# Experts layers: turned, weighed selections built by VectorE from repeated rows instead of by TensorE transposes

## The reference, cut to what matters

```
scores = einsum('BTC,CE->BTE', layernorm(x), gate_w)        # E = 8 experts
probs_et = transpose(softmax(scores), (0, 2, 1))
top_p, top_idx = top_k(probs_et, 64)                        # 64 tokens per expert and batch
xin = take_along_axis(x, top_idx)
y = gelu(xin @ w1[e]) @ w2[e]                               # 128 -> 512 -> 128
out = zeros.at[b_idx, top_idx].add(y * top_p)
```

## Time and profile before

| | |
|---|---|
| executions, us | 2262.53, 2264.82, 2267.56 |
| profiled execution, us | 2265.85 (its span 2264.1, clock granted on average 0.943) |
| PE busy | 2009.0 us, 89% of the span |
| DVE, ACT, POOL busy | 1573.0, 1174.4, 857.1 us |
| first experts block, first to last work | 643.7 to 855.3 us |
| second experts block, first to last work | 1107.2 to 1324.9 us |

### The profile page before, as it was taken

How to read it: one execution, slowest core, us unless ns; L and a number is a source line. 1 busy time by engine, 2 the same in 40 slices (tenths; PEclk the granted TensorE clock), 3 DMA queues, 4 the chain that set the end, 5 groups by cost and what they waited for, 6 DMA issues and landing times. The chain is left out here.

```text
span 2264.1 us, 55096 instructions
## 1 busy us (share of the span) xinstructions
PE 2009.0 (89%) x21847; PEld 1339.1 (59%) x21847; DVE 1573.0 (69%) x2826; ACT 1174.4 (52%) x1968; POOL 857.1 (38%) x1361
## 2 busy tenths in 40 slices
PE   5999999999979997999698979997599985479996
PEld 2666666666658994665498966664355542335553
DVE  5777778777866425667654447775689975769994
ACT  4444444444333334666433226666478875448874
POOL 4444544545434422344233424440244323333340
PEclk9999999999989997999799989999699997769998
DMA  5000000000000012443000214440334320123431
GB/s 173 1 1 2 1 1 1 2 1 2 1 7 5 16 42 73 123 116 98 5 1 1 57 38 124 117 117 19 87 105 117 108 61 0 44 81 112 119 108 51
DMA packets 157394, 121.18 MB, mean 54 GB/s; under 512 B 14113, under 2 KB 129713, under 8 KB 157141
## 3 DMA queue, kind: packets, MB, share of 16 engines
q1 hardware_dynamic: 157140, 117.65, 18.6%
HBM read 63.48 MB, written 54.12 MB: 52 GB/s over the span
## 5 line engine op out<-in xcount | busy, mean ns | idle before, releaser
L1269 DVE TENSOR_REDUCE l_group_mx<-maxima 128x4 f32<-128x1024 f32 x248 | 304.0, 1226 | 52.4 <-PE maxima L1056 50.9
L1194 ACT ACTIVATE l_group_pr<-scores 128x1024 f32<-128x1024 f32 x256 | 261.7, 1022 | 70.7 <-PE scores L1077 68.1
L2450 POOL TENSOR_TENSOR l_wide_tiles_sum<-l_wide_pr 128x256 f32<-128x256 f32 x256 | 180.8, 727 | 200.1 <-ACT l_wide_pr L2389 199.9
L2419 DVE RECIPROCAL l_wide_rc<-bank 128x256 f32<-128x256 f32 x128 | 224.1, 1751 | 6.1 <-PE bank L2346 4.4
L2389 ACT ACTIVATE l_wide_pr<-scores 128x512 f32<-128x512 f32 x256 | 139.0, 594 | 160.3 <-PE scores L2329 160.3
L2403 DVE TENSOR_REDUCE l_wide_mx<-maxima 128x2 f32<-128x512 f32 x248 | 159.2, 684 | 42.5 <-PE maxima L2309 42.4
L1269 DVE TENSOR_REDUCE l_slope_mx<-maxima 128x6 f32<-128x768 f32 x124 | 118.9, 959 | 65.6 <-PE maxima L1063 64.5
L2379 ACT ACTIVATE l_wide_qk<-bank 128x512 f32<-128x512 f32 x128 | 76.4, 597 | 155.5 <-PE bank L2293 155.5
L1269 DVE TENSOR_REDUCE l_rope_mx<-maxima 128x6 f32<-128x768 f32 x124 | 118.8, 958 | 43.8 <-PE maxima L1063 42.8
L1194 ACT ACTIVATE l_slope_pr<-scores 128x768 f32<-128x768 f32 x128 | 103.6, 810 | 75.0 <-PE scores L1084 74.9
L1097 PE MATMUL bank<-l_group_pr,va 128*32 128x256 f32 x2048 | 142.2, 397 | 0.0
(11 more groups left out here) (577 smaller groups left out, 4838.6 us busy)
## 6 DMA issues: line engine op xcount, KB each, us to landing
l_group_st<-stack_dram SPq DMA_DIRECT2D x128, 192.0 KB, 3.3
l_slope_st<-stack_dram SPq DMA_DIRECT2D x64, 192.0 KB, 3.7
l_rope_st<-stack_dram SPq DMA_DIRECT2D x64, 192.0 KB, 3.8
stack_dram<-l_group_parts SPq DMA_DIRECT2D x64, 192.0 KB, 2.3
stack_dram<-l_group_parts SPq DMA_DIRECT2D x64, 128.0 KB, 1.9
...
```

The source lines that it names most:

```text
L1194: act.activation(pr[:, i % AHEAD, :, 0:keys], Tp[:, :, 0:keys], ACT.Exp).then_inc(s["exps"], 1)
L1269: dve.tensor_reduce(mx[:, b % 2, :, :, i], max_bank(i, b)[:, :, 0:BLOCKS * keys].rearrange("p z (a k) -> p z a k", k=keys), AX.X, ALU.max, ...
L2419: own.done(dve.reciprocal(rc[:], Ob[i % 2][:, S:2 * S]))
L2450: pool.tensor_tensor(tiles_sum[:, i % 2, z, :], pr[:, i % 2, z, 0:S], pr[:, i % 2, z, S:2 * S], ALU.add).then_inc(s["added"], 1)
```

## The change

The turned selections are no longer transposed. The places (as bf16) and the probabilities of each half, 64 rows of 256 tokens each, are stored to DRAM (`rstore`). For each unit SP repeats its rows over 64 partitions each (`fetch`, four DMAs), and two DVE instructions (`build`, slots 6 and 8) compare the repeated places with the number of the partition and multiply with the probability. `turn`, `late` and the multiplications on POOL are gone. `gpt` and the two fetched tiles exist once, so a fetch waits for the builds of the unit before, and a build waits for the fetch and for the scatter of the unit before.

```diff
@@ expert_schedule
-    if n >= 0:
-        a.update({4: [("turn", 0)], 5: [("turn", 1)], 6: [("turn", 2)], 7: [("turn", 3)]})
-    late = {3: [("late", 0), ("late", 1)], 8: [("late", 2), ("late", 3)]} if n == 0 else {}
+    build = {6: [("build", 0)], 8: [("build", 1)]}
@@ experts, sync
+            def fetch(unit):
+                wait(sp, s["weighed"], 2 * unit)
+                for u in range(U):
+                    rows = slice((U * unit + u) * E8, (U * unit + u + 1) * E8)
+                    to = slice(u * CAP, (u + 1) * CAP)
+                    sp.dma_start(unit_place[to].rearrange("p e s -> p (e s)"),
+                                 K.place_dram[rows].rearrange("e s -> (e s)").partition_broadcast(CAP)).then_inc(s["fetched"], 16)
+                    sp.dma_start(unit_prob[to].rearrange("p e s -> p (e s)"),
+                                 K.prob_dram[rows].rearrange("e s -> (e s)").partition_broadcast(CAP)).then_inc(s["fetched"], 16)
+            for unit in range(3):
+                fetch(unit)
+            for i in range(2):
+                routed.sp(sp, "rstore", i)
+            fetch(3)
             following.sp_first(sp)
-            following.first("sp", sp, 5 * HOSTED)
+            fetch(4)
+            following.first("sp", sp, 5)
+            fetch(5)
+            following.first("sp", sp, 5)
+            fetch(6)
+            fetch(7)
@@ experts, tensor
-                    elif what in ("turn", "late"):
-                        if i == 0:
-                            pe.wait_ge(s["weighed"], weighed_t.add(4))
-                        for j in range(4):
-                            ins = pe.transpose(bank[:, j * P:(j + 1) * P], gp[...], K.ident[:])
-                        ins.then_inc(full[b], 1)
...
                         pe.wait_ge(s["kept"], kept_t.add(2))
+                        pe.wait_ge(s["weighed"], 2 * n)
@@ experts, scalar
+            act.activation(routed.greatest[:, 0:1], K.rstd[:, 0:1], ACT.Gelu)
             normed(act, 1).then_inc(s["xn"], 1)
-            routed.root(act)
@@ experts, vector
+                    elif what == "build":
+                        if i == 0:
+                            dve.wait_ge(s["fetched"], 16 * 2 * U * (n + 1))
+                            wait(dve, s["scattered"], n)
+                        of = slice(4 * i, 4 * i + 4)
+                        dve.scalar_tensor_tensor(gpt[:, of], unit_place[:, of], number[:], unit_prob[:, of],
+                                                 ALU.is_equal, ALU.mult).then_inc(s["weighed"], 1)
@@ Route
+    def root(self, pool):
+        pool.tensor_tensor(self.K.rstd[:, tiles], self.K.var[:, tiles], self.power[:], ALU.pow).then_inc(self.s["root"], 1)
+    def sp(self, sp, what, i):
+        if i == 0:
+            self.copied(sp, "rby", 0)
+            sp.dma_start(K.prob_dram[rows], self.work[0][0:64]).then_inc(s["kept_prob"], 16)
+        else:
+            sp.wait_ge(s["place16"], 1)
+            sp.dma_start(K.place_dram[rows], self.place16).then_inc(s["kept_place"], 16)
...
+            if i == 3:                                   # rtop.3
+                dve.wait_ge(s["kept_prob"], 16)
...                                                      # rplace.3
+            dve.tensor_copy(self.place16, self.place).then_inc(s["place16"], 1)
@@ ROUTE_IN_WIDE
-    (12, 1, "rby.0"),
-    (12, 2, "rtop.0"),
+    (14, 1, "rby.0"),
+    (15, 0, "rtop.0 rtop.1 rtop.2"),
@@ ROUTE_IN_EXPERTS
-    (-1, 3, "rstat.0 rnorm.0 rnorm.1"),
+    (0, 1, "rstat.0"),
```

More of the change, by code:

```diff
@@ L302, in norm @@
             if i == 0:
[L303 to L304 removed]
+                own.done(eng.memset(self.power[:], -0.5))
                 own.done(eng.memset(self.gate[:], 0.0))
@@ L316, in norm @@
                 own.done(eng.tensor_tensor(rstd, var, self.power[:], ALU.pow))
+                self.shifts(eng, tiles, own)
             else:
                 eng.sem_inc(s["var"], 1)
-                eng.wait_ge(s["root"], 1)
-                own.done(eng.reciprocal(rstd, rstd))
-            own.done(eng.tensor_tensor(shift, mean, rstd, ALU.mult))
-            eng.tensor_scalar(shift, shift, -1.0, None, ALU.mult).then_inc(s["norm"], 1)
+        elif what == "rshift":
+            eng.wait_ge(s["root"], 1)
+            self.shifts(eng, slice(NT * ROUTED * self.half, NT * ROUTED * (self.half + 1)), own)
         elif what == "runit":
@@ L508 @@
     (9, 3, "rback.0"),
-    (10, 5, "rstat.1"),
-    (10, 7, "rnorm.4"),
-    (11, 0, "rnorm.5"),
-    (11, 1, "rturn.2"),
-    (11, 5, "rnorm.6"),
-    (11, 6, "rnorm.7"),
-    (12, 1, "rturn.3"),
-    (12, 2, "rgate.1"),
-    (12, 3, "rback.1"),
-    (12, 5, "rsoft.0"),
-    (12, 7, "rsoft.1"),
-    (13, 1, "rby.0"),
-    (13, 5, "rtop.0"),
-    (13, 7, "rtop.1"),
-    (14, 0, "rtop.2"),
-    (14, 1, "rtop.3"),
-    (14, 5, "rtop.4"),
-    (14, 7, "rtop.5"),
-    (15, 0, "rtop.6"),
-    (15, 1, "rtop.7"),
@@ L529 @@
[L529 to L543 removed]
+    (12, 6, "rstat.1"),
+    (12, 7, "rnorm.4"),
+    (13, 0, "rnorm.5"),
+    (13, 1, "rturn.2"),
@@ new lines @@
+    (13, 5, "rnorm.6"),
+    (13, 6, "rnorm.7"),
+    (14, 1, "rturn.3"),
+    (14, 2, "rgate.1"),
+    (14, 3, "rback.1"),
+    (14, 5, "rsoft.0"),
+    (14, 7, "rsoft.1"),
+    (15, 1, "rby.0"),
+    (15, 1, "rtop.0 rtop.1"),
+    (15, 2, "rtop.2 rtop.3"),
+    (15, 3, "rtop.4 rtop.5"),
+    (15, 4, "rtop.6 rtop.7"),
+    (15, 5, "rtop.8 rtop.9"),
+    (15, 6, "rtop.10 rtop.11"),
+    (15, 7, "rtop.12 rtop.13"),
+    (16, 0, "rtop.14 rtop.15"),
+    (16, 1, "rplace.0 rplace.1 rplace.2 rplace.3"),
@@ L555 @@
-    (1, 3, "rback.1 rsoft.0"),
-    (1, 4, "rsoft.1"),
-    (1, 8, "rby.0"),
-    (2, 0, "rtop.0"),
-    (2, 0, "rtop.1"),
-    (2, 1, "rtop.2"),
-    (2, 1, "rtop.3"),
-    (2, 2, "rtop.4"),
-    (2, 2, "rtop.5"),
-    (2, 3, "rtop.6"),
-    (2, 3, "rtop.7"),
+    (0, 1, "rstat.0"),
+    (0, 2, "rroot.0"),
+    (0, 4, "rshift.0"),
+    (0, 5, "rnorm.0 rnorm.1"),
+    (0, 8, "rturn.0"),
+    (1, 0, "rnorm.2 rnorm.3"),
+    (1, 1, "rturn.1"),
+    (1, 2, "rnorm.4 rnorm.5"),
+    (1, 3, "rgate.0 rturn.2"),
@@ L566 @@
+    (1, 4, "rback.0"),
+    (1, 5, "rnorm.6 rnorm.7"),
+    (1, 7, "rturn.3"),
+    (1, 8, "rgate.1"),
+    (2, 0, "rback.1 rsoft.0"),
+    (2, 1, "rsoft.1"),
+    (2, 2, "rby.0"),
+    (2, 2, "rtop.0"),
+    (2, 2, "rtop.1"),
+    (2, 2, "rtop.2"),
+    (2, 3, "rtop.3"),
+    (2, 3, "rtop.4"),
+    (2, 3, "rtop.5"),
+    (2, 4, "rtop.6"),
+    (2, 4, "rtop.7"),
     (2, 4, "rtop.8"),
-    (2, 4, "rtop.9"),
+    (2, 5, "rtop.9"),
     (2, 5, "rtop.10"),
@@ L571 @@
     (2, 6, "rtop.13"),
-    (2, 7, "rtop.14"),
+    (2, 6, "rtop.14"),
     (2, 7, "rtop.15"),
-    (2, 8, "rplace.0 rplace.1 rplace.2 rplace.3 rslot.0"),
+    (2, 7, "rplace.0 rplace.1 rplace.2 rplace.3"),
+    (2, 8, "rslot.0"),
 ])
@@ L755, in narrow_walk @@
     routed = ROUTE_IN_SLOPE if kind == "slope" else {}
-    for n in range(-max(ahead), NB - min(ahead)):
+    last = max([NB - min(ahead)] + [n + 1 for n, _ in routed])
+    for n in range(-max(ahead), last):
         for j, slot in enumerate(at):
@@ L1729, in expert_schedule @@
             pieces += e.get(slot, [])
-        pieces += late.get(slot, [])
+        if do_b:
+            pieces += build.get(slot, [])
         if n < 0:
@@ L1921, in step @@
                     b, filling = bank_of(fill, what, i)
-                    if what in ROUTE_ON and what in ("rstat", "rnorm"):
+                    if what in ("rstat", "rnorm", "rshift"):
                         routed.norm(dve, what, i, routed.own_norm.on(dve))
@@ L1967, in _ @@
             pool.tensor_copy(count[:], count_i[:]).then_inc(s["counted"], 1)
+            pool.wait_ge(s["counted"], 2)
+            for u in range(U):
+                wait(pool, s["numbered"], u)
+                pool.iota(number_i[u * CAP:(u + 1) * CAP], pattern=[[1, 1]], base=0, channel_multiplier=1).then_inc(s["numbered"], 1)
+            pool.wait_ge(s["numbered"], U)
+            pool.tensor_copy(number[:], number_i[:]).then_inc(s["numbered"], 1)
             def step(n, par, do_a, do_b, do_e):
@@ L1989, in _ @@
             pool.wait_ge(s["in_three"], 1)
-            batches(pool, [onehot_t], step, UNITS)
+            batches(pool, [], step, UNITS)
 def recurrent(nc, K, name, W):
```

121 lines of the change are left out of this document (48 added, 73 removed).

## The result

| | before | after |
|---|---|---|
| executions, us | median 2265.41 (2262.53 to 2267.56, 4 runs) | median 2237.69 (2232.76 to 2238.64, 4 runs) |
| ratio to before | | 0.9874, 95% interval 0.9859 to 0.989 |
| profiled execution, us | 2265.85 (span 2264.1, clock 0.943) | 2238.64 (span 2236.9, clock 0.944) |

A forecast was written before the change was run, and what follows sets the result against it. The prediction took PE to bound plain experts steps, DVE step 2 and the attention ends. Its terms, -28.4 - 11.8 - 8.4 + 4.0 + 1.6 + 1.0 + 3.4 + 0.7 = -37.9, gave 2227 us from 2264.8; own range 2219 to 2236, with rivals 2213 to 2244.

The forecast's parts named there:

- its own signs of being wrong: Steps 3 and 4 don't shrink, PE waits for `weighed` at a scatter, or DVE waits for fetches outside steps 5 and 6.
- The transposes: Between down and up in both experts blocks: 0.444 us of PE per group, all counted as gain, -28.4 us.
- The fetches of steps 5 and 6: Issued on SP behind the hosted stacks, they may hold builds past their slot: +0.5 us per block, +1.0.
- Rival B: Fetches of steps 5 and 6 and the stacks sharing SP hold scatter, 4 us in four steps: 2243 us, chance 0.06.
- Start of a block: Statistics and root leave step -1, so ACT copies at once and the first `up` comes 5.9 us earlier: -11.8 for both.
- step 0: First step of each experts block: 26.3 us falls to 18.5; beyond the transposes, -4.2 per block, -8.4 us.
- rival C: Full clock from the first `up`, no wait in step 1, faster selections: 6 us more per block, 2215 us, chance 0.13.
- Step 1: Takes in 1.2 us of routing on PE and a 0.8 us wait for ACT's copy: +4.0 us for both blocks.
- Step 2: DVE's ranking chain starts later; first block's step 25.1 us against 26.1, +0.8 per block beside the transposes' gain, +1.6.
- End of `wide`: Fourteen rankings and a cast move into the last batch, so the last division ends later: +3.4 us.
- End of `slope`: Six rankings, `rby` and a cast go into a last batch where DVE idled: +0.7 us, 0 to 3.6.
- Rival A: Moved routing costs what it was meant to hide, in steps 1 and 2, attentions and start: 2244 us, chance 0.15.

The follow-up runs named there:

- no_turns: The kernel before with PE's transposes and their DVE copies left out, nothing in their place: 2228.8 us, 35.9 less than before.
- turns_back: The changed kernel with transposes and POOL's multiplications put back, no fetch or build, routing still late: 2257.8 us, 7.6 less than before.
- fetch_first: The changed kernel with the fetches of units 5 and 6 issued on SP ahead of the hosted stacks: 2228.8 us, 8.9 less than the changed kernel.
- wide_fetch: The changed kernel with each fetch DMA bringing half the first batch's rows to 128 partitions, same bytes; second batch gets the first's weights: 2229.1 us.
- stat_early: The changed kernel with POOL's piece of the hosted statistics in step 3 moved ahead of its splitting of the normed x: 2232.2 us.
- combined: The changed kernel with early fetches, POOL's early statistics and both builds of step 2 behind the places: 2217.6 us, 20.1 less than the changed kernel.
- old_route: The changed kernel with the second half's routing back at its old places from step -1, root staying on POOL: 2254.3 us, 16.7 more.
- route_tight: The changed kernel with routing's pieces one to three slots earlier and the ranking from slot 0 of step 2: 2243.5 us, 5.8 more.
- dense: The changed kernel with early fetches and POOL's early statistics, all sixteen rankings and the places together ahead of step 2's kept copy: 2225.1 us.
- weights_later: The combined kernel with hosted weights moved from step 2 to step 3 and constant rows issued behind unit 4's fetch: 2215.5 us, 2.1 less than combined.

## Why the forecast was right in kind and 11 us off in size

The range held (2213 to 2244) and the direction came from the named places, but the forecast's own case was 2227 (2219 to 2236), and two of its own signs of being wrong came: step 4 did not shrink, and PE waited for builds at scatters. That the sum is off by no more than 11 us is in part luck: the front of the blocks gained more than forecast, and what the transposes cost was underrated (35.9, not 28.4), while late builds and the attentions took more than that back.

1. **The transposes** (-28.4). The work on PE was sized rightly: 1.7 us less per plain step, 1.78 forecast. The sentence "they stand between down and up with nothing late behind them" failed on both sides. Before, their copies were part of a wait of PE at the end of step 3 (1.22 us and a lower clock), which went too. After, the builds, which replace them on DVE, were late enough to hold PE at two places of the first block and three of the second. no_turns gives 35.9 for the transposes with nothing in their place, turns_back 20.1 for the change of one for the other.
2. **The fetches of steps 5 and 6** (+1.0). This is the term that failed, the mis-sized one: fetch_first puts it at 8.9. Rival B had the mechanism and the place, with 0.06. Two numbers were wrong. A fetch took 10.1 us with nothing ahead of it and 11.8 behind the stacks, not 7.4. A row of a transfer to all 128 partitions was the measure for four to 64; by wide_fetch that is 1.9 of the 2.7 us, and 0.8 stay unexplained. The stacks ahead, which the forecast left out of the fetch's time, add the other 1.7. And the wait was priced by when the fetch lands, not by what stands behind the build on the in-order DVE: two builds, the kept copy, the selections of the next unit.
3. **A wait that was in the trace of before and not priced**: DVE stood 3.63 us behind POOL's piece at the end of step 3. With step 3 shorter it became 5.20, and the build behind it made it PE's: 5.4 us in the two steps 4, of which stat_early alone keeps 1.7 in the blocks and combined all.
4. **Start of a block** (-11.8) and **step 0** (-8.4 and its transposes): right in mechanism, 12.8 us for the starts of the blocks from first selection to first `up` (POOL's index rows, which the forecast counted here, stand before it and take back 0.7 per block), and 17.4 us for step 0 against 18.5. The granted clock is 1.00, 2.4 GHz, from the first `up` on, as rival C had it.
5. **Step 1** +0.7 against +0.4, with 0.50 us of PE's wait for the copy of `rgate.0` where 0.8 was taken. **Step 2**: 26.5 us against 25.1. The wait for the places was 3.99, not 2 to 3. While POOL split the normed x, a build took 1.45 us and one small piece 1.22, where in the second block they took 1.28 and 0.28, the small piece after POOL had ended.
6. **End of `wide`** (+3.4): 1.2. **End of `slope`** (+0.7) with POOL's index rows: 1.4. The second attention was 2.9 us longer; 1.0 of it stands in front of a batch's first scores (a wait of 0.70 us for a stack), 1.3 in its last 20 us, where the granted clock was 0.83 for 10 us. From the experts' end to the next layer that stretch took 246 to 249 us among these kernels, whose instructions there are the same, and no run was made for it: it stays open, and it can blur a difference of medians of a few us.

Rival A (the moved routing costs what it hides) is refuted by old_route: undone, it costs 16.7 us. What bounds step 2 is settled only in part: starting the ranking earlier (old_route, route_tight) did nothing to the wait, because a kept copy that waits for PE stands in the middle of it; taking a build from before the places gave 1.6 to 1.8 per block, and reordering alone (dense) moved the wait. The remaining 2.6 us are not the hosted weights'; by the trace of weights_later the ranking's own 12.2 us behind the turned probabilities are left, 1.1 of them POOL's, which no run tested. No run turned the probabilities earlier with no kept copy in the way.
